# The last attention of a two-layer block taken one token tile at a time, with softmax sums from the value matmul

## The reference

```python
def _L1_xattn_ref(q, k, v, mask, Wq, bq, Wk, bk, Wv, bv, Wo, bo):
    ...
    qh, kh, vh = (proj(q, Wq, bq), proj(k, Wk, bk), proj(v, Wv, bv))   # 16 heads of 16
    scores = jnp.einsum('bhqd,bhkd->bhqk', qh, kh) / jnp.sqrt(jnp.float32(D_K))
    scores = jnp.where(mask == 0, jnp.float32(-1000000000.0), scores)
    attn = jax.nn.softmax(scores, axis=-1)                             # over 64 keys
    x = jnp.einsum('bhqk,bhkd->bhqd', attn, vh)
    ...
    return x @ Wo.T + bo
```

## Time and profile before

| | us |
|---|---|
| median of 3 runs | 852.84 (851.17 to 852.88) |
| the profiled execution | 846.41 |
| its span | 844.6 |
| busy in the span: TensorE, weight loads, VectorE, ScalarE, GpSimd | 770.9, 628.6, 449.7, 255.3, 190.2 |
| this stage, 538 to 653 us of the span | 115 |

### The profile page before, as it was taken

One profiled execution on the slowest core, in us unless ns is written; L12 is line 12 of the kernel. 1 busy time (PEld: TensorE's weight loads), 2 busy tenths in 40 slices (PEclk: granted clock), 3 DMA queues, 4 the chain that ended last, 5 costly groups with the idle time before them and its releaser, 6 DMA issues.

```text
span 844.6 us, 11374 instructions
## 1 busy us (share of the span) xinstructions
PE 770.9 (91%) x4207; PEld 628.6 (74%) x4207; DVE 449.7 (53%) x866; ACT 255.3 (30%) x500; POOL 190.2 (23%) x180
## 2 busy tenths in 40 slices
PE   5998999978989999999999999978786599999996
PEld 4665766667878878887888787745565499999995
DVE  3574679987923862386239532797957411111111
ACT  1643314221212221122112212465542233333331
POOL 3012343652000200020002000465531212222221
PEclk9999999989999999999999999999987699999999
DMA  9963500005000000000000000090122667666640
GB/s 328 376 203 125 224 0 1 1 0 200 2 2 2 3 2 2 2 2 3 2 2 2 2 2 2 2 396 3 51 73 78 239 230 221 224 208 216 203 145 0
DMA packets 20525, 79.69 MB, mean 94 GB/s; under 512 B 3053, under 2 KB 12400, under 8 KB 15664
## 3 DMA queue, kind: packets, MB, share of 16 engines
q1 hardware_dynamic: 17504, 70.44, 24.2%
q0 software_dynamic: 2944, 8.13, 2.5%
HBM read 72.27 MB, written 18.74 MB: 108 GB/s over the span
## 4 chain that ended last, share of the span: by engine, by line
PE 68%; DVE 19%; issue 6%; ACT 2%; DMA 2%; POOL 2%; DVEq 0%; SPq 0%; POOLq 0%; ACTq 0%
PE ps L1081 30%; PE ps L1780 9%; PE ps L1768 9%; PE ps L493 3%; PE ps L528 2%; DVE stats L282 2%; DVE head_max L1610 2%; DVE f_ha_hi L1182 1%; DVE f_raw L1176 1%; PE ps L479 1%; PE ps L557 1%; PE ps L1220 1%; DVE c_tok L1611 1%; DVE head_sum L1619 1%; DVE a_tok L844 1%
## 5 line engine op out<-in xcount | busy, mean ns | idle before, releaser
L1159 ACT ACTIVATE f_raw<-ps,cols 128x512 f32<-128x512 f32 x96 | 66.2, 690 | 256.9 <-PE ps L1081 234.6
L1081 PE MATMUL ps<-f_hb_hi,fh 128*128 128x512 f32 x256 | 101.2, 395 | 2.5 <-DVE inexact L327 2.5
L1081 PE MATMUL ps<-f_ha_hi,fh 128*128 128x512 f32 x256 | 99.9, 390 | 2.3 <-ACT f_raw L1159 2.3
L1081 PE MATMUL ps<-f_hb_lo,fh 128*128 128x512 f32 x256 | 100.6, 393 | 0.0
L1081 PE MATMUL ps<-f_ha_lo,fh 128*128 128x512 f32 x256 | 99.6, 389 | 0.0
L1768 PEld LDWEIGHTS ps<-xsT,ew 128*128 128x128 f32 x736 | 87.1, 195 | 3.1 <-DVE xsT L1895 2.0
L1768 PE MATMUL ps<-xsT,ew 128*128 128x128 f32 x736 | 87.5, 278 | 1.4 <-DMA ew<-in_ew 0.9
L1828 ACT ACTIVATE hT<-ps,ew 128x128 f32<-128x128 f32 x184 | 52.5, 369 | 106.4 <-PE ps L1768 97.4
L1780 PE MATMUL ps<-ew,hT 128*128 x368 | 83.2, 380 | 0.0
L1182 DVE CAST f_ha_hi<-f_raw 128x512 fp32r<-128x512 f32 x64 | 33.1, 517 | 89.4 <-ACT f_raw L1159 88.3
L1780 PEld LDWEIGHTS ps<-ew,hT 128*128 128x128 f32 x368 | 68.2, 190 | 8.5
(11 more groups left out here) (235 smaller groups left out, 1339.9 us busy)
## 6 DMA issues: line engine op xcount, KB each, us to landing
ew<-in_ew SPq DMA_DIRECT2D x23, 1028.0 KB, 5.8
fh<-fh_copy SPq DMA_DIRECT2D x2, 4096.0 KB, 14.8
ew<-in_ew SPq DMA_DIRECT2D x1, 8192.0 KB, 23.4
fw<-fw_copy SPq DMA_DIRECT2D x3, 1024.0 KB, 7.0
eb<-in_eb SPq DMA_DIRECT2D x23, 128.0 KB
x_res<-in_x SPq DMA_DIRECT2D x4, 512.0 KB, 10.9
rows<-x_res SPq DMA_DIRECT2D x4, 512.0 KB, 3.4
rows<-xn_e SPq DMA_DIRECT2D x4, 512.0 KB, 3.1
```

Of the source, the lines that this page charges most:

```text
L1081: ins = nc.tensor.matmul(out, *((xk, wk) if swap else (wk, xk)), start=(k == 0 and part == 0), stop=(k == w.shape[1] - 1 and part == 1))
L1159: nc.scalar.activation(f_raw[:, m % 3, :], ps[:, ring_bank(n), :], ACT.Silu if m < KH else ACT.Gelu, scale=col(("w1_s", "h1_s", "h2_s")[m ...
```

## The change

The stage is worked tile by tile. The sums of softmax are no longer taken on VectorE, and the division comes after the values.

- VectorE subtracts the maxima as before, into one buffer. TensorE transposes these logits of one tile, four pairs of heads to a bank, and ScalarE's copy out of PSUM is the exponential (`exponentials`, two instructions of 512 columns per tile).
- `heads(n)`: for each of the 8 pairs of heads one matmul whose stationary operand is that pair's 128 keys x 128 tokens of c_pT; moving are 32 columns of values and 2 of ones (v1_blocks is now 34 wide). The result, in bank 6, is token-major: heads and sums.
- `scale_heads(n)`, VectorE: reciprocal of the 16 sums and a product of 256 columns, both out of PSUM, into c_heads_tok. TensorE transposes that twice (`head_columns`) and ScalarE copies it to c_oT; `project(n)` follows, always in bank 7.
- `exponential`, `invert_sum`, `divide`, and VectorE's part of the copies are gone. A turn i of the loop holds `scores(i)`, `head_columns(i-3)`, `project(i-3)`, `probabilities(i-1)`, `heads(i-2)`. Behind the loop, the last projections and the gate work of batches 0 to 2 stand in a new order on TensorE and VectorE.

```diff
+HEAD_COLS = 2 * DH1 + 2
...
-            def heads(b):
-                pe.wait_ge(c_values, NG1 * (b + 1))
-                pe.wait_ge(c_pT_even, PAIR_EVEN * (b + 1))
-                pe.wait_ge(c_pT_odd, PAIR_EVEN * (b + 1))
+            def heads(n):
+                b, j = divmod(n, TT)
+                if j == 0:
+                    pe.wait_ge(c_values, values_done(b))
+                pe.wait_ge(c_pT_out, 2 * (n + 1))
+                if n:
+                    pe.wait_ge(c_heads, n)
...
+                for a in range(PAIRS1):
+                    o, q = divmod(a, TT)
+                    m = q // 2 * TT + 2 * o + q % 2
+                    ins = nc.tensor.matmul(ps[:, 6, a * HEAD_COLS:(a + 1) * HEAD_COLS], c_pT[:, m, j * P:(j + 1) * P],
+                                           v1_blocks[:, b % 2, a, :], start=True, stop=True)
+                ins.then_inc(c_pv_full, 1)
+
+            def head_columns(n):
+                pe.wait_ge(c_heads, n + 1)
+                if n:
+                    pe.wait_ge(c_wo_taken, n)
                 for o in range(NG1):
...
+                    ins = nc.tensor.transpose(ps[:, 7, o * P:(o + 1) * P], c_heads_tok[:, n % 2, o * P:(o + 1) * P],
+                                              ident)
+                ins.then_inc(c_hT_full, 1)
...
-            for b in range(B):
-                scores(b, 0)
-                scores(b, 1)
-                if b < LAST:
+            for i in range(NT):
+                b, j = divmod(i, TT)
+                next_columns = j == 1 and b < LAST
+                scores(b, j)
+                if i >= 3:
+                    head_columns(i - 3)
+                if next_columns:
                     attn1_columns(pe, b + 1)
...
+                if j == 2 and b < LAST:
+                    probabilities(i - 2)
+                if i >= 3:
+                    project(i - 3)
+                if i and not next_columns:
+                    probabilities(i - 1)
+                if i >= 2:
+                    heads(i - 2)
+                if next_columns:
                     attn1_queries(pe, b + 1)
...
-            def exponential(b, j):
-                act.wait_ge(c_sub, TT * b + j + 1)
-                nc.scalar.activation(c_tok[b % 2][:, j], c_tok[b % 2][:, j], ACT.Exp).then_inc(c_exp, 1)
-
...
+                for h in range(2):
+                    act.wait_ge(c_pT_full, 2 * n + h + 1)
+                    nc.scalar.activation(c_pT[:, h * TT:(h + 1) * TT, j * P:(j + 1) * P],
+                                         ps[:, h, :].rearrange("p (m n) -> p m n", m=TT), ACT.Exp).then_inc(c_pT_out, 1)
...
+                if next_columns:
                     attn1_columns_out(act, b + 1)
...
                     attn1_queries_out(act, b + 1)
...
+                    if b + 2 < B:
+                        rows_in(b + 2)
+                if j == 2 and b < LAST:
+                    exponentials(i - 2)
+                if i and not next_columns:
+                    exponentials(i - 1)
...
+                s_order.step(nc.vector.reciprocal(sums, out_[:, :, 2 * DH1:]))
...
+            for i in range(NT):
+                if i >= 3:
+                    scale_heads(i - 3)
+                subtract_max(*divmod(i, TT))
+                if i >= 3:
+                    residual(*divmod(i - 3, TT))
```

More of the change, by code:

```diff
@@ L1351, in heads @@
-            def heads(b):
-                pe.wait_ge(c_values, NG1 * (b + 1))
-                pe.wait_ge(c_pT_even, PAIR_EVEN * (b + 1))
-                pe.wait_ge(c_pT_odd, PAIR_EVEN * (b + 1))
-                for o in range(NG1):
-                    for q in range(TT):
-                        ins = nc.tensor.matmul(ps[q * 2 * DH1:(q + 1) * 2 * DH1, o, :],
-                                               v1_blocks[:, b % 2, o * TT + q, :],
-                                               c_pT[:, q // 2 * TT + 2 * o + q % 2, :], start=True, stop=True)
-                    ins.then_inc(c_pv_full, 1)
@@ L1362, in project, with probabilities @@
-            def project(b, j):
-                n = b * TT + j
-                if j == 0:
-                    pe.wait_ge(c_pv_out, NG1 * (b + 1))
-                if n >= 2:
-                    pe.wait_ge(c_wo_taken, n - 1)
+            def probabilities(n):
+                b, j = divmod(n, TT)
+                pe.wait_ge(c_sub, n + 1)
+                if j == 0 and b < LAST:
+                    pe.wait_ge(c_q_out, NG1 * (b + 2))
+                for h in range(2):
+                    if n:
+                        pe.wait_ge(c_pT_out, 2 * (n - 1) + h + 1)
+                    for m in range(TT):
+                        heads = c_tok[:, j, 8 * h + 2 * m:8 * h + 2 * m + 2, :].rearrange("p a k -> p (a k)")
+                        ins = nc.tensor.transpose(ps[:, h, m * P:(m + 1) * P], heads, ident)
+                    ins.then_inc(c_pT_full, 1)
@@ L1461, in attn1_tensor @@
+            head_columns(NT - 3)
+            probabilities(NT - 1)
+            project(NT - 3)
+            heads(NT - 2)
             gate_columns(0)
-            project(B - 2, 2)
-            project(B - 2, 3)
+            head_columns(NT - 2)
+            heads(NT - 1)
+            project(NT - 2)
             gate_logits(0)
-            probabilities(LAST, 0, 4)
             gate_columns(1)
-            probabilities(LAST, 4, 2)
+            head_columns(NT - 1)
             gate_logits(1)
-            probabilities(LAST, 6, 2)
+            project(NT - 1)
@@ L1511, in rows_out, with exponentials, head_columns @@
                                          bias=shift_out[:, t:t + 1]).then_inc(c_xn, 1)
[L1513 to L1524 removed]
+            def exponentials(n):
+                j = n % TT
+                if n >= TT:
+                    act.wait_ge(c_pv_full, n - TT + 1)
+                for h in range(2):
+                    act.wait_ge(c_pT_full, 2 * n + h + 1)
+                    nc.scalar.activation(c_pT[:, h * TT:(h + 1) * TT, j * P:(j + 1) * P],
+                                         ps[:, h, :].rearrange("p (m n) -> p m n", m=TT), ACT.Exp).then_inc(c_pT_out, 1)
+            def head_columns(n):
+                j = n % TT
+                act.wait_ge(c_hT_full, n + 1)
+                if n >= TT:
+                    act.wait_ge(c_wo_full, n - TT + 1)
+                nc.scalar.activation(c_oT[:, :, j * P:(j + 1) * P], ps[:, 7, 0:D].rearrange("p (o n) -> p o n", o=NG1),
+                                     ACT.Identity).then_inc(c_hT_out, 1)
             def gate_columns(b):
```

223 lines of the change are left out of this document (70 added, 153 removed).

## The result

| | before | after |
|---|---|---|
| median over all runs of this comparison | 852.86 (851.17 to 854.49, 4 runs) | 878.39 (870.55 to 879.91, 4 runs) |
| the profiled execution | 846.41 | 879.91 |
| start of the stage (first scores) | 538.25 | 542.69 |
| last `g_e` | 651.22 | 684.74 |
| the stage between the two | 112.97 | 142.05 |

All times in us. The ratio after to before is 1.0282, 95% interval 1.0255 to 1.0309. The forecast was 862.8 with a range of 854 to 869: the sign is right, the size is not, and the time lies outside the range. Of the 33.5 us between the two profiled executions, 4.4 lie ahead of the stage, in code that did not change; the stage itself is 29.1 us longer where the forecast said 10.0; what follows it is the same.

A forecast was written before the change was run, and what follows sets the result against it. VectorE was taken to bound batches 1 to 3, then a mixed chain at clock 0.83, with TensorE becoming the bound. The terms put the last g_e at 661.2 against 651.22: 852.8 + 10.0 = 862.8 us, range 854 to 869.

The forecast's parts named there:

- The step that failed: In the stage's sum, TensorE was taken to run at 2.4 GHz throughout up to 649 us.
- the start's wait: TensorE's idle time ahead of transposes(1), waiting for the first exponential, near 548 to 551 us: 2.6 us.
- half clock stays: Rival: as many half-clock microseconds in the stage as before, 20, add up to 7 us: 869 us; chance 0.14.
- Start: First term: from the first scores to the end of heads(0) at 553.6 us, with a TensorE wait of 2.6 us.
- Turns 3 to 15: Second term, the loop: nine ordinary turns 50.9, turns 5 and 6 15.4, turns 9 and 10 14.5; together 80.8 us.
- The turn itself: TensorE's ordinary loop turn: scores 1.18, head transposes 0.24, wait 0.65, projection 0.87, transposes 0.94, heads 1.78; 5.66 us.
- the rival of cheap short matmuls: Rival: heads stay near 0.46 us a tile, giving 844 us, deciding from 1.15; with other such gains, chance 0.10.
- VectorE in a turn: VectorE's work in each loop turn: 4.4 us, covered by TensorE with 1.2 us to spare.
- Behind the loop: Third term: last scaling wait, heads, projections, gate transposes and logits to the end of project(15): 15.1 us, to 649.5.
- Routing: Fourth term: from residual(15) to the last g_e, 11.7 us where before took 7.64, ending at 661.2.
- The order's cost: In routing, TensorE holds gate_logits(2) behind ranks_inside(1); VectorE waits 0.3 + 1.78 and 0.2 us to land.
- nothing changes: After the stage, behind 661 us, the kernel was to stay as before.

The follow-up runs named there:

- e3_wide: Kernel after with 64 moving columns instead of 34 in the heads' matmuls, the added ones zeros: 867.47 us, ratio 1.0189.
- e6_twice: Kernel after with the start's wait mended and each of a tile's 8 heads matmuls done twice, 34 moving columns: 924.68 us, ratio 1.0888.
- e10_twice_wide: As e6_twice, but with 64 moving columns instead of 34 in each heads matmul: 893.02 us, ratio 1.0466.
- e1_filler: Kernel after with 22 constant transposes on TensorE while it waits for the first exponential: 866.89 us, ratio 1.0182.
- e8_gate: Kernel after with first exponential early, 64 moving columns in heads and gate logits, batch 2's gate logits ahead of batch 1's ranks: 859.39 us, ratio 1.0117.
- e4_tail: Kernel after with the gate logits of batch 2 put ahead of the ranks of batch 1 on TensorE: 875.35 us, ratio 1.0293.
- e7_sums: Kernel before with the exponential in ScalarE's copy, sums from matmuls with ones, and VectorE dividing feature-major: 877.15 us, ratio 1.0306.
- e9_before_fill: Kernel before with 104 constant transposes in TensorE's waits of batches 1 to 3: 848.06 us, ratio 0.9937.

## Why the prediction was wrong, step by step

**The step that failed** is the sentence "My sum takes 2.4 GHz throughout up to 649 us, since turns leave TensorE idle only 0.65 us at a time." The stage has 45.4 us of half clock, the first 27 of them between 557 and 585 us; the prediction itself had named more than 10 us before 640 as what would refute it. Two things were wrong in it. It took idle time for the only cause, read off one place of before; e3_wide against after shows that the same wait costs no half clock when the work behind it is wider, e6_twice against e10_twice_wide that thin matmuls bring the clock down without a long wait, and the change had just made a third of TensorE's turn thin. And it put the start's wait, which it had found and sized (2.6, measured 2.43), down as 2.6 us, when it was to cost 14: e1_filler fills this wait, gains nothing from the filling itself, and is 11.8 us shorter in the stage. The sign did not come out by luck: e8_gate, without half clock in the stage, is still 1.2% slower than before.

**The rival that came closest**, "half clock stays", had half of the mechanism, the idle time at the start, and was under-sized. It took the half-clock time of before, 20 us, and 7 us for it, where the stage has 45.4. At the price that e1_filler and after show (11.8 us for 26.7) that is 20 us. Its counter-argument, "TensorE is nearly gapless in the loop", is the one that the runs contradict.

By the terms of the sum (the stage was to be 122.95 us, and is 142.05):

- *Start*, 15.35 forecast, 15.92 measured; the 0.6 are the first heads, half of them at 1.2 GHz. Right, with the cause as told: in ScalarE's timeline `x_in` 2.06, table load 1.28, and the first exponential behind them.

```profile
551.21 2.06 ACT L1500 ACTIVATE x_in<-x_res,shift_in,rstd_all 128x256 f32<-128x256 f32 x4
553.29 1.28 ACT L1515 ACT_TABLE_LOAD   x1
554.58 1.09 ACT L1515 ACTIVATE c_pT<-ps 128x512 f32<-128x512 f32 x2
```

- *Turns 3 to 15*, 80.8 forecast, 94.2 measured (558.61 to 652.82, where the heads of tile 13 end: 651.01 and 1.81). Of the 13.4 more, 1.6 are nine ordinary turns of 5.84 us where 5.66 were forecast; the rest is the first stretch of half clock.
- *The turn itself.* Heads 1.81 (601.43 to 603.24) against 1.78: the term that decided the sign was right, and the rival of cheap short matmuls is refuted, its 1.15 us far off. Wait with head transposes 0.91 (598.68 to 599.59) against 0.89: the transposes took 0.44 and the wait 0.47. Scores 1.28 against 1.18 and projection 0.97 against 0.87 were each 0.1 short. The scores had been read where a second group of scores follows (596.30 to 596.51 in before, 0.21 us behind the start of the mask's matmuls; in after the next group starts 0.31 us behind it). The projection had been read where no wait stands ahead of it; there it takes 0.87 in after too (620.10 to 620.97). Transposes 0.87 against 0.94.
- *VectorE in a turn.* The forecast was 1.2 us of idle time, covered by TensorE. Its timeline after:

```profile
603.34 0.26 DVE L1612 RECIPROCAL head_sum<-ps 128x16 f32<-128x16 f32 x1 [0.73 <-PE ps L1360]
603.63 0.42 DVE L1613 TENSOR_TENSOR c_heads_tok<-ps,head_sum 128x256 f32<-128x256 f32 x1
604.62 1.23 DVE L1602 TENSOR_REDUCE head_max<-ps 128x16 f32<-128x1024 f32 x1 [0.57 <-PE ps L1331]
```

  0.73 and 0.57, 1.3 us. The reciprocal is 0.26 and the product 0.42, as costed.
- *Behind the loop*, 15.1 forecast, 18.25 measured (652.82 to residual(15) at 671.07). Up to 663 it went to plan, with the wait for scaling 0.81 for a forecast 1.0; then the clock falls, right behind a group of gate logits with 8 moving columns.

```profile
661.31 1.85 PE L1401 MATMUL ps<-gate_w,g_xT 128*128 128x8 f32 x16
663.01 1.84 PE L1391 MATMUL ps<-const,xn_e 128*128 128x128 f32 x8
...
665.54 3.59 PE L1401 MATMUL ps<-gate_w,g_xT 128*128 128x8 f32 x16 [0.26 <-ACT g_xT L1531]
```

  The same gate logits take 1.70 us at 661.31 and 3.44 at 665.54, and again the fall stands behind thin work, with no wait since 653.69.
- *Routing*, 11.7 forecast, 13.67 measured (671.07 to 684.74). The order's cost came as told: VectorE waits for batch 2's logits, 3.02 us where 2.3 were forecast, again at half clock.

```profile
671.07 0.42 DVE L1624 TENSOR_TENSOR x_res<-x_res,ps 128x256 f32<-128x256 f32 x1 [5.95 <-PE ps L1377]
...
678.81 0.19 DVE L1637 TENSOR_TENSOR g_e<-ps,rows 128x32 f32<-128x32 f32 x1 [3.02 <-PE ps L1401]
```

These four differences are 0.6, 13.4, 3.1 and 2.0, together the 19.1 us by which the stage missed its forecast. About 17 of them are clock, by the estimate of some 125 us for this stage without half clock that e8_gate gives. The median missed by less, 15.6 us, since it was forecast from 852.8 and not from the fast execution in the trace.

**Behind the stage**, "nothing changes" was right (193.36 against 193.38).

**What stays open.** Why the profiled execution of before began the stage at 538.25, when all others of the study did so at 540.3 to 543.1 with the same code ahead: between 150 and 300 us its granted clock is 0.97, in after 0.95, which accounts for about 3 us; what decides that from one execution to the next was not tried. And e4_tail's profiled execution had a first stretch of half clock 13 us shorter than that of after without any cause in the code; so what a single trace says of such a stretch is good to some 6 us (13 at the price of 11.8 for 26.7). The fourth run of after, 8 us faster than the others at a clock of 0.961 instead of 0.95, says the same without a trace. What decides when the clock falls and how long it stays down is not known from these runs, only that idle time and thin work both bear on it.

## What to carry to other kernels

A matmul with a full stationary operand and few moving columns was paid twice here: by its weight load, and by TensorE's clock, which can fall during it though the timeline has no gap. Where a change makes work thin, price the stage at half clock too, and look for any idle time just ahead of the thin work; filling it with constant transposes, or padding the moving side from 34 to 64 columns, which the weight load still hid, cost nothing that shows and gave 11 to 12 us here, each by itself. Look at the granted clock of all runs before a single trace is believed. And before the price of a wait is written down as its own length, ask what the clock does behind it.

## What the runs showed of the hardware that was not expected

- **Half clock without a gap.** Eight matmuls of 128x128 float32 with 34 moving columns, done twice a tile, leave 73 us of the stage at 1.2 GHz (e6_twice); with 64 columns 17.5, all behind the loop (e10_twice_wide). The Trainium skill ("TensorE: Matmul & The Clock Gate", section "What's actually happening") says that the gate follows how busy TensorE has been recently. By the busy time that the profile shows these rows do not agree: it is 1.00 in the microsecond ahead of the fall in e6_twice.
- **Columns that cost nothing.** 1.81 us for eight matmuls of 34 columns (after), 1.83 for 64 (e3_wide), and 1.70 to 1.78 for 8 (gate logits of after and before), all at full clock. What the three have in common is a weight load of 128x128 float32 each, and that is what seems to set them.
- **Reciprocal on VectorE goes by the element.** 253 ns for 16 columns and 3358 ns for 512 (e7_sums), so about 6.3 ns a column between them, where the product of 512 columns beside it took 0.69 us in all. The Trainium skill ("VectorE: DVE Perf Modes", section "First, the fixed hardware budget") says that it is an iterated divide with a repeat count of 8; the trace agrees with the direction, at about five times the product's time.
- **Waits of TensorE were worth filling even where it did not bind.** 104 constant transposes in its waits made the kernel before 0.6% faster (e9_before_fill), in batches that VectorE bounds.
- **A wait is not always followed by the same clock.** The same start with the same wait of 2.4 us had 27.3 us of half clock behind it in the trace of after and 13.7 in that of e4_tail.
